# A decoder with a mixture of experts on one core: a second copy of late samples' rows for the scatter, joins of two samples at once, and the last products of the weights' quantization on GpSimd

## The chip, the core and the metric

The kernel runs on one core of a Trainium2 chip. Its engines are TensorE (PE, with PEld for its weight loads), VectorE (DVE), ScalarE (ACT), GpSimd (POOL) and SyncE (SP), which only issues DMAs. The metric is the device time of one execution in microseconds (us); the median of several runs counts.

## The reference, cut to what matters

Sixteen samples of 128 tokens x 256 features (f32) go through six sub-layers, with a layer norm after each. Only the last one is a mixture of experts; the change touches its routing, its output, and the preparation of the third one's weights.

```python
x = norm(x + L0_attn(x))         # a linear recurrence with decay per head
x = norm(x + L0_xattn(x, ctx))   # 16 heads, RoPE, softmax
x = norm(x + L0_ffn(x))          # weights and activations rounded to FP4 in blocks of 16
x = norm(x + L1_attn(x))         # linear attention, then a 1024-wide GELU network
x = norm(x + L1_xattn(x, ctx))   # 16 heads, softmax
x = norm(x + L1_ffn(x))          # 8 experts, the top 2 of each token:

probs = softmax(xf @ gate_w + gate_b)            # xf: 2048 x 256
gates, expert = top_k(probs, 2)
h = relu(xf @ w1[e] + b1[e])                     # 512 wide
expert_out = h @ w2[e] + b2[e]
out = sum over the two experts of gate * expert_out

def fp4_quant_dequant(x):                        # blocks of 16 values
    scale = max(|x|) / 6
    return nearest(x / scale in the grid 0, .5, 1, 1.5, 2, 3, 4, 6) * scale
```

## The kernel before

**Slots and the planner.** A sample lives in one of six slots (sample n in slot n % 6). The work of a sample is cut into pieces. Each piece names what it needs and gives its expected time on each engine (the functions `plan_*`; "D" is DVE, "A" and "a" are ACT, "P" and "p" are GpSimd, "S" is SP, "Q" and "L" are a DMA's time in the queue and its latency). When the program is built, a planner plays these pieces through greedily and writes down in which order each engine takes them. Each engine then runs its instructions strictly in that order, and waits on semaphores where an input isn't there. A changed cost or need in any `plan_*` can so move pieces of any sample on any engine.

**First stage.** The weights of the FP4 network are quantized in nine parts of 512 or 384 columns (`dve_weights`, `pool_weights`). For each, DVE finds the blocks' scales and rounds (L1062 is the small operation on the scales, 128x32); the last product with the scale goes to DVE for the five even parts (`dve_fp4_scale`, L1073) and to GpSimd for the four odd ones. Samples start while this goes on.

**Middle.** All engines work on several samples at a time. ACT's activations need function tables that are loaded on a change of function: L1447 is the exponential of attention, L1529 and L1534 belong to the GELU network, L1491 to the FP4 network's gate. An ACT_TABLE_LOAD in the trace or in the program order is such a change.

**Router.** For a sample n, PE transposes its finished rows X6, DVE and ACT make the softmax and the top 2, and PE counts ranks with two small matmuls (L988, L989); from these DVE makes two rows of destinations (`idx`, L1304), one for each expert. GpSimd then writes the 128 rows with an indirect DMA to `xs_d`, a buffer in HBM sorted by expert (`pool_router`, L1753). A row is 258 wide: 256 features, where its result has to go ("dest"), and its gate. For the second expert the same 128 rows are written again (`pool_second`, L1765), but dest and gate differ. Both copies would read the same tile X6, so GpSimd waits until the first scatter has landed, rewrites the two columns (L1762, L1763), and then issues the second.

**Expert tiles.** After samples 8, 12 and 16 a table says how many rows each expert has. The expert work is cut into tiles of 128 rows: 17 tiles are done between the samples' pieces and 22 behind the last table. A tile takes 1 MB of weights by two DMAs (L1899, L1903) and its rows by one (L1894), all issued by SP. On PE it is a transpose (`turn`, L710), an up product (8 x 128x128 matmuls in two chunks, L705 with EW as the second operand) and a down product (4 of 128x256). Eight weight loads of the last step are issued before its rows. They stand on SP behind the saving of sample 14 (`sp_bias`), which holds the gated b2 (L1359, a DVE add on X6, which has to wait until both scatters of the sample have read X6).

**Join.** When all tiles are stored, `join_turns` goes through the 16 samples: SP fetches 384 KB (two expert rows and x6 of each token, L1873), GpSimd adds the first (L1775), DVE adds the second (L1371) and computes mean and variance (L1373 to L1376), GpSimd takes the root (L1635), ACT centres and scales (L1598, L1602), SP writes the result (L1876).

## Time and profile before

| | us |
|---|---|
| three runs | 997.7, 997.95, 1003.37 |
| their median | 997.95 |
| the profiled execution | 995.66 |
| its span in the trace | 993.6 |
| busy in the span: PE, PEld | 869.8, 691.2 |
| busy: DVE, ACT, POOL | 619.7, 488.5, 289.8 |

The profiled execution took 2.1 us more than its span, and 2.3 us less than the median. The program has four stretches in the trace: the preparation to about 100 us, the samples with the first 17 tiles to about 840, the gap about the last sample's router to 872, and the last 22 tiles with the join behind them. PE is busy nine tenths and more of nearly every fortieth of the span but the first ones, the one at 845 to 870, and the last.

### The profile page before, as it was taken

How to read it: one execution, taken by the hardware profiler on the slowest of the kernel's cores; microseconds unless marked ns; L12 is line 12 of the kernel's file. 1: busy time of each engine (PE TensorE's matmuls, PEld its weight loads, DVE VectorE, ACT ScalarE, POOL GpSimd, SP SyncE). 2: the span in 40 equal slices, each digit the busy share in tenths (PEclk: the TensorE clock that was granted, in tenths of full speed). 3: DMA queues.
4: the chain of work that ended last, by engine and by line, in shares of the span. 5: the costliest groups of instructions: out<-in, count | busy, mean ns of one | idle time of the engine just before them, and what ended most of it. 6: DMA issues, size and time to landing. Idle time of an engine off the chain costs nothing.

```text
span 993.6 us, 19713 instructions
## 1 busy us (share of the span) xinstructions
PE 869.8 (88%) x7316; PEld 691.2 (70%) x7316; DVE 619.7 (62%) x1845; ACT 488.5 (49%) x1150; POOL 289.8 (29%) x473
## 2 busy tenths in 40 slices
PE   3569999989988989999999999999999999599950
PEld 2346777668766756767777887777677888489940
DVE  4999887674771798977755778767974444200016
ACT  1335545435446646455564555565444555145535
POOL 4313322111340143422121333322421123312236
PEclk9679999999998999999999999999999999889985
DMA  9996000000010000000000003321230036899836
GB/s 325 402 321 210 2 2 12 12 1 14 25 34 12 17 28 28 18 6 6 12 12 17 18 28 119 107 81 42 72 107 28 28 119 192 317 320 343 321 122 242
DMA packets 35950, 102.33 MB, mean 103 GB/s; under 512 B 4984, under 2 KB 20352, under 8 KB 35296
## 3 DMA queue, kind: packets, MB, share of 16 engines
q1 hardware_dynamic: 32448, 91.74, 27.1%
q0 software_dynamic: 3408, 9.34, 2.5%
q8 instruction: 58, 0.95, 0.4%
q14 instruction: 36, 0.29, 0.1%
HBM read 87.53 MB, written 33.35 MB: 122 GB/s over the span
## 4 chain that ended last, share of the span: by engine, by line
PE 70%; DVE 14%; ACT 6%; issue 4%; DMA 3%; POOL 2%; SPq 0%; ACTq 0%; DVEq 0%; POOLq 0%
PE ps L705 49%; PE ps L710 8%; PE ps L717 6%; PE ps L781 3%; DMA xs_d<-X,idx 2%; DVE PT L1109 2%; ACT PT L1447 2%; DVE stat L1045 1%; PE ps L848 1%; ACT slot_rows L1447 1%; PE ps L882 1%; DMA KB<-xs_d 1%; DVE sm L1061 1%; DVE PT L1096 1%; PE ps L891 1%
## 5 line engine op out<-in xcount | busy, mean ns | idle before, releaser
L1635 POOL TENSOR_TENSOR stat<-stat,mhalf 128x1 f32<-128x1 f32 x112 | 65.9, 589 | 322.3 <-DVE stat L1047 322.1
L705 PE MATMUL ps<-wall,slot_rows 128*128 128x256 f32 (+1 forms) x448 | 134.5, 425 | 10.1 <-ACT KB L1474 8.3
L705 PEld LDWEIGHTS ps<-wall,slot_rows 128*128 128x128 f32 x448 | 78.8, 194 | 32.7 <-issue 20.9
L1109 DVE TENSOR_REDUCE PT<-ps 128x8 f32<-128x1024 f32 x64 | 75.3, 1219 | 29.8 <-PE ps L717 29.8
L717 PE MATMUL ps<-KB 32*128 32x128 f32 (+1 forms) x2048 | 78.2, 290 | 10.4 <-ACT slot_rows L1447 3.5
L717 PEld LDWEIGHTS ps<-KB 32*128 32x128 f32 (+1 forms) x2048 | 66.0, 192 | 29.5 <-issue 25.7
L710 PE MATMUL ps<-cst,PT 128*128 128x128 f32 x512 | 75.5, 284 | 11.1 <-DVE PT L1109 4.1
L705 PE MATMUL ps<-wgu,slot_rows 128*128 128x352 f32 x256 | 81.0, 470 | 2.1 <-ACT PT L1452 0.8
L710 PEld LDWEIGHTS ps<-cst,PT 128*128 128x128 f32 x512 | 60.8, 146 | 27.3 <-issue 13.8
L705 PE MATMUL ps<-slot_rows,wall 128*128 128x128 f32 x640 | 78.4, 277 | 0.3 <-DVE slot_rows L1119 0.2
L705 PEld LDWEIGHTS ps<-slot_rows,wall 128*128 128x128 f32 x640 | 74.7, 192 | 4.0 <-issue 0.9
L705 PEld LDWEIGHTS ps<-wgu,slot_rows 128*128 128x128 f32 x256 | 48.4, 193 | 29.5 <-issue 3.3
L1409 ACT COPY slot_rows<-ps 128x256 f32<-128x256 f32 x96 | 35.7, 378 | 60.2 <-PE ps L710 59.8
L705 PE MATMUL ps<-wall,cT 128*128 128x512 f32 x128 | 64.3, 627 | 0.0
L705 PE MATMUL ps<-wall,PT 128*128 128x256 f32 x256 | 59.6, 386 | 1.7 <-ACT KB L1432 1.7
L705 PEld LDWEIGHTS ps<-wall,PT 128*128 128x128 f32 x256 | 48.3, 193 | 9.7 <-ACT KB L1432 2.0
L1701 POOL TENSOR_TENSOR KB<-PT,sm 128x352 f32<-128x352 f32 x32 | 26.1, 817 | 84.9 <-DVE PT L1069 84.7
L1045 DVE BATCH_NORM_STATS2 stat<-slot_rows 128x6 f32<-128x256 f32 x112 | 47.9, 428 | 3.8
L705 PE MATMUL ps<-wdn,PT 128*128 128x256 f32 x192 | 47.3, 388 | 0.0
L705 PE MATMUL ps<-EW,work 128*128 128x256 f32 x184 | 43.9, 381 | 2.4 <-DMA EW<-moe_w 1.4
L705 PE MATMUL ps<-work,EW 128*128 128x128 f32 x368 | 45.2, 276 | 0.9 <-DVE PT L1109 0.5
L705 PEld LDWEIGHTS ps<-work,EW 128*128 128x128 f32 x368 | 43.0, 192 | 1.6 <-DVE PT L1109 0.7
(237 smaller groups left out, 1803.8 us busy)
## 6 DMA issues: line engine op xcount, KB each, us to landing
EW<-moe_w SPq DMA_DIRECT2D x23, 514.0 KB, 4.2
EW<-moe_w SPq DMA_DIRECT2D x23, 512.0 KB, 5.1
PT<-moe_w SPq DMA_DIRECT2D x12, 514.0 KB, 5.5
PT<-moe_w SPq DMA_DIRECT2D x12, 512.0 KB, 6.5
wall<-wts SPq DMA_DIRECT2D x1, 4104.0 KB, 19.8
work<-xs_d SPq DMA_DIRECT2D x25, 129.0 KB, 2.7
KB<-ys_d SPq DMA_DIRECT2D x8, 384.0 KB, 6.2
slot_rows<-ys_d SPq DMA_DIRECT2D x8, 384.0 KB, 9.3
```

The source lines that it names most:

```text
L705: last = k.e.matmul(o, a, b, start=(i == 0), stop=(i == len(pairs) - 1))
L710: last = k.e.transpose(ps[:, u.at, c * P:(c + 1) * P], src[:, c * P:(c + 1) * P], ident)
L717: last = k.e.matmul(ps[:, at, c * P:(c + 1) * P], lhsT[lane, c * P:(c + 1) * P], rhs[lane, c * P:(c + 1) * P], start=True, stop=True)
L781: last = k.e.matmul(ps[lane:lane + HR, u.at, c:c + P], VS[:, s, h * (DH + 1):h * (DH + 1) + HR], exps(s, a, i // HC)[:, i % HC * P:(i % HC ...
L848: last = k.e.transpose(ps[0:kw[i], u.at + i // 4, (i % 4) * P:(i % 4 + 1) * P], KB[s][:, i * P:i * P + kw[i]], ident)
L882: last = k.e.matmul(o[:, c, :], AT[:, s, c * P:(c + 1) * P], V1(s)[:, c, :], start=True, stop=True)
L1045: k.after(k.step(e.bn_stats(v[:, 0:6], src)))
L1109: e.tensor_reduce(peak[:, 2 * p:2 * p + 2, :, DH], s4, AX.X, ALU.max).then_inc(emptied[u.at], 1)
L1409: k.e.copy(dst, v3(ps[:, u.at, 0:D], P)).then_inc(emptied[u.at], 1)
L1447: e.activation(v3(exps(s, a, p), 512), ps[:, u.at:u.at + 2, :], ACT.Exp, scale=DH ** -0.5).then_inc(emptied[u.at], 1)
L1635: return k.e.tensor_tensor(v[:, 7:8], v[:, 8:9], mhalf[:, :], ALU.pow)
L1701: e.tensor_tensor(h, y, bc(sm[:, s, j, 1, 0:m].unsqueeze(2), m, DH), ALU.mult).then_inc(gpsimd[s], 1)
```

## The change

It has three parts and a consequence.

1. **Weights.** GpSimd makes the last product of all nine parts; before it made four.

```diff
                 dve_fp4_head(k, part, width, tmp, small, wxn_ready)
                 yield
                 k.wait_ge(wabs_ready, i + 1)
-                if i % 2:
-                    dve_fp4_tail(k, tmp).then_inc(wy_ready, 1)
-                else:
-                    k.after(k.step(dve_fp4_tail(k, tmp)))
-                    dve_fp4_scale(k, part, width, tmp, small).then_inc(wq_even, 1)
+                dve_fp4_tail(k, tmp).then_inc(wy_ready, 1)
                 yield
...
         def pool_weights(k):
             for i, (f, lo, width) in enumerate(wq_parts):
                 yield
-                if i % 2:
-                    m = width // DH
-                    part, y = v3(raw[f][0][:, lo:lo + width], DH), v3(wq_part(i, width)[1], DH)
-                    k.wait_ge(wy_ready, i // 2 + 1)
-                    k.e.tensor_tensor(part, y, bc(ws[:, 1, 1, 0:m].unsqueeze(2), m, DH), ALU.mult).then_inc(wq_odd, 1)
+                m = width // DH
+                part, y = v3(raw[f][0][:, lo:lo + width], DH), v3(wq_part(i, width)[1], DH)
+                k.wait_ge(wy_ready, i + 1)
+                k.e.tensor_tensor(part, y, bc(ws[:, i % 2, 1, 0:m].unsqueeze(2), m, DH), ALU.mult).then_inc(
+                    wq_odd if i % 2 else wq_even, 1)
                 yield
```

2. **Router.** Samples 12 to 15 (TWIN) get a second copy of their row, in the space of slots 4 and 5 (`twin_rows`), which samples 10 and 11 (DONE) must have left. ACT copies the 256 features, GpSimd writes the two other columns, and both scatters are issued one behind the other. `pool_second` stays for samples 0 to 11. The copy of "dest" moves to the start of the router's work.

```diff
         def act_router(k):
             for n in range(B):
                 act_copy(k, U[n]["x6T"], x6T[:, :, :])
+                if n in TWIN:
+                    k.wait_ge(vector[slot(n)], count(VECTOR, n, "normed", 6))
+                    for m in DONE:
+                        k.wait_ge(vector[slot(m)], count(VECTOR, m, "normed", 6))
+                    k.e.copy(twin_rows(n)[:, 0:D], X6[:, slot(n), 0:D]).then_inc(twinned, 1)
                 yield
...
+        def pool_scatter(k, n, i, rows_):
+            k.e.indirect_dma_start(xs_d, bass.IndirectOffsetOnAxis(ap=idx[:, n, i:i + 1], axis=0), rows_,
+                                   None).then_inc(scattered[slot(n)], 16)
 
         def pool_router(k):
             for n in range(B):
-                yield
-                yield
-                yield
-                k.wait_ge(zeroed, 16 * len(zero_parts))
-                k.wait_ge(idx_ready, n + 1)
                 if n >= NS:
                     k.wait_ge(scattered[slot(n)], sent(n - NS))
                 k.e.tensor_copy(X6[:, slot(n), D:D + 1], k_("dest")[:, 2 * n:2 * n + 1]).then_inc(directed, 1)
+                if n in TWIN:
+                    for m in DONE:
+                        k.wait_ge(vector[slot(m)], count(VECTOR, m, "normed", 6))
+                    k.e.tensor_copy(twin_rows(n)[:, D:D + 1], k_("dest")[:, 2 * n + 1:2 * n + 2]).then_inc(twin_tail, 1)
+                yield
+                yield
+                if n in TWIN:
+                    k.wait_ge(picked, 2 * n + 1)
+                    k.e.tensor_copy(twin_rows(n)[:, D + 1:XW], mx8[:, n, 1:2]).then_inc(twin_tail, 1)
+                yield
+                k.wait_ge(zeroed, 16 * len(zero_parts))
                 k.wait_ge(directed, n + 1)
-                k.e.indirect_dma_start(xs_d, bass.IndirectOffsetOnAxis(ap=idx[:, n, 0:1], axis=0), X6[:, slot(n), :],
-                                       None).then_inc(scattered[slot(n)], 16)
+                k.wait_ge(idx_ready, n + 1)
+                pool_scatter(k, n, 0, X6[:, slot(n), :])
+                if n in TWIN:
+                    k.wait_ge(twinned, n - TWIN[0] + 1)
+                    k.wait_ge(twin_tail, 2 * (n - TWIN[0]) + 2)
+                    pool_scatter(k, n, 1, twin_rows(n))
                 yield
                 for t in step_at(n):
                     yield
```

3. **Join.** The 16 samples are joined in ten groups: six of two samples and four of one (samples 0, 7, 14, 15). GpSimd's add, DVE's add, the root and DVE's two small operations take a group at once; DVE's statistics and ACT's steps stay one for each sample. The buffer of statistics has a place for each sample.

```diff
+GROUPS = [range(0, 1), range(1, 3), range(3, 5), range(5, 7), range(7, 8), range(8, 10), range(10, 12), range(12, 14), range(14, 15),
+          range(15, 16)]
+
+TWIN = range(B - 4, B)
+DONE = range(B - 6, B - 4)
...
-            for what, n in join_turns():
+            for what, g in join_turns():
                 if what == "join":
-                    v, rows_ = mv2[:, n % 8, :], join_rows(n)
...
+                    n, (y1, y2, x6) = GROUPS[g], joined_rows(g)
+                    v = mv2[:, n[0]:n[-1] + 1, :]
+                    k.wait_ge(halved, g + 1)
+                    e.tensor_tensor(x6, x6, y2, ALU.add).then_inc(joined, 1)
+                    k.wait_ge(joined, g + 1)
+                    for i in range(len(n)):
+                        stats = k.step(e.bn_stats(v[:, i, 0:6], x6[:, i, :]))
+                    k.after(stats)
+                    for i in range(len(n)):
+                        aggr = k.step(e.bn_aggr(v[:, i, 6:8], v[:, i, 0:6]))
+                    k.after(aggr)
+                    e.tensor_scalar(v[:, :, 8:9], v[:, :, 7:8], 1e-5, None, ALU.add).then_inc(var6, 1)
+                    e.tensor_scalar(v[:, :, 6:7], v[:, :, 6:7], -1.0, None, ALU.mult).then_inc(var6, 1)
                 yield
...
                 if what == "add":
-                    rows_ = join_rows(n)
-                    x6 = rows_[:, 2 * D:3 * D]
-                    k.wait_ge(fetched[n], 16)
-                    k.e.tensor_tensor(x6, x6, rows_[:, 0:D], ALU.add).then_inc(halved, 1)
+                    y1, y2, x6 = joined_rows(g)
+                    for n in GROUPS[g]:
+                        k.wait_ge(fetched[n], 16)
+                    k.e.tensor_tensor(x6, x6, y1, ALU.add).then_inc(halved, 1)
                 elif what == "join":
-                    k.wait_ge(var6, 2 * n + 2)
-                    pool_root(k, mv2[:, n % 8, :]).then_inc(root6, 1)
+                    n = GROUPS[g]
+                    v = mv2[:, n[0]:n[-1] + 1, :]
+                    k.wait_ge(var6, 2 * g + 2)
+                    k.e.tensor_tensor(v[:, :, 7], v[:, :, 8], bc(mhalf[:, :], len(n)) if len(n) > 1 else mhalf[:, :],
+                                      ALU.pow).then_inc(root6, 1)
                 yield
```

4. **The planner's numbers** follow:

```diff
-        yield piece(work=[("D", 1.4, None), ("P", 1.2, ("wq", i)) if i % 2 else ("D", 0.7, ("wq", i))],
+        yield piece(work=[("D", 1.4, None), ("P", 1.2, ("wq", i))],
...
-        yield piece(0.25, [(n, "x6T")], [("A", 0.36, (n, "x6T"))], [(n, "done", 1)], True)
+        twin = n in TWIN
+        yield piece(0.25, [(n, "x6T")], [("A", 0.36, (n, "x6T")), ("p", 0.2 + 0.2 * twin, None), *[("a", 0.5, None)] * twin],
+                    [(n, "done", 1), *[(m, "done", 1) for m in DONE] * twin], True)
...
-        yield piece(work=[("D", 2.05, (n, "routed"))], needs=[("f", n - 2, "gT")] * (n > 1))
-        yield piece(0.4, [(n, "rank")], [("D", 0.78, (n, "rank")), ("P", 1.16, None), ("Q", 0.5, None),
-                                         ("L", 2.4, (n, "half sent"))])
+        yield piece(work=[("D", 2.05, (n, "routed")), *[("p", 0.2, None)] * twin], needs=[("f", n - 2, "gT")] * (n > 1))
+        yield piece(0.4, [(n, "rank")], [("D", 0.78, (n, "rank")), ("P", 1.0, None), ("Q", 0.5, None),
+                                         ("L", 2.4, (n, "half sent"))] if n not in TWIN else
+                    [("D", 0.78, (n, "rank")), ("P", 1.9, None), ("Q", 0.5, None), ("L", 2.6, (n, "sent"))])
         for t in step_at(n):
...
 def plan_second():
-    for n in range(B):
+    for n in range(TWIN[0]):
         yield piece(work=[("P", 1.4, None), ("Q", 0.5, None), ("L", 2.4, (n, "sent"))], needs=[(n, "half sent")], alone=True)
```

Since these feed the planner, the order of the instructions changes on all engines. On ACT the program had 49 ACT_TABLE_LOADs and has 61. One place of it, before (L1529 and L1534: GELU network; L1447: attention's exponential; L1464, L1441, L1409, L1421: copies that need no table of their own):

```order
L1529 ACT_TABLE_LOAD
L1529 ACTIVATE PT<-ps,col 128x128 x8
L1464 ACTIVATE slot_rows<-ps,col 128x128 x2
L1534 ACTIVATE slot_rows<-slot_rows 128x256
L1529 ACTIVATE PT<-ps,col 128x128 x8
L1441 COPY KB<-ps 128x512
L1409 COPY slot_rows<-ps 128x256 x2
L1421 COPY VS<-ps 128x16x16
L1534 ACTIVATE slot_rows<-slot_rows 128x256
L1447 ACT_TABLE_LOAD
```

After (the lines have moved: L1543 and L1548 are the GELU network, L1461 the exponential):

```order
L1548 ACTIVATE slot_rows<-slot_rows 128x256
L1461 ACT_TABLE_LOAD
L1461 ACTIVATE PT<-ps 128x1024
L1461 ACTIVATE slot_rows<-ps 128x1024
L1543 ACT_TABLE_LOAD
L1543 ACTIVATE PT<-ps,col 128x128 x8
L1461 ACT_TABLE_LOAD
L1461 ACTIVATE PT<-ps 128x1024
L1461 ACTIVATE slot_rows<-ps 128x1024
L1466 COPY PT<-ps 128x512
L1423 COPY slot_rows<-ps 128x256
L1435 COPY VS<-ps 128x16x16
```

Four changes of table stand where one stood: GELU pieces and exponentials alternate.

PE about the last sample's router, before. The transpose of X6 is that of sample 15, "x6T 128x8" its logits, L988 and L989 its ranks; "work,EW" is an up product and "EW,work" a down product of an expert tile:

```order
L710 MATMUL ps<-cst,X6 128x128 x2
L1000 MATMUL ps<-cst,gates 8x128
L705 MATMUL ps<-work,EW0 128x128 x8
L705 MATMUL ps<-wall,x6T 128x8 x2
L705 MATMUL ps<-EW1,work 128x256 x4
L710 MATMUL ps<-cst,work 128x128 x2
L988 MATMUL ps<-mask,cst 128x8
L989 MATMUL ps<-mask,ones 128x8
L705 MATMUL ps<-work,EW1 128x128 x8
L705 MATMUL ps<-EW0,work 128x256 x4
L705 MATMUL ps<-work,EW0 128x128 x8
L1006 MATMUL ps<-b2m,gT 128x256
```

After (L726 is L705, L731 is L710, L1009 and L1010 are the ranks); the first pair of ranks is sample 14's, the second sample 15's:

```order
L1009 MATMUL ps<-mask,cst 128x8
L1010 MATMUL ps<-mask,ones 128x8
L731 MATMUL ps<-cst,X6 128x128 x2
L1021 MATMUL ps<-cst,gates 8x128
L726 MATMUL ps<-EW1,work 128x256 x4
L726 MATMUL ps<-wall,x6T 128x8 x2
L731 MATMUL ps<-cst,work 128x128 x2
L726 MATMUL ps<-work,EW1 128x128 x8
L726 MATMUL ps<-EW0,work 128x256 x4
L1009 MATMUL ps<-mask,cst 128x8
L1010 MATMUL ps<-mask,ones 128x8
L726 MATMUL ps<-work,EW0 128x128 x8
```

One more up product and one more down product of expert tiles stand ahead of the last ranks (the 8 x 128x128 and the 4 x 128x256 ones that were behind them).

GpSimd for samples 14 and 15, before ("X6<-cst" writes dest, "X6<-mx8" the gate):

```order
L1751 COPY X6<-cst 128x1
L1753 DMA xs_d<-X6,idx 19200x258
L1787 DMA ys_d<-work,place 7168x256
L1762 COPY X6<-cst 128x1
L1763 COPY X6<-mx8 128x1
L1765 DMA xs_d<-X6,idx 19200x258
L1751 COPY X6<-cst 128x1
L1753 DMA xs_d<-X6,idx 19200x258
L1787 DMA ys_d<-work,place 7168x256
L1762 COPY X6<-cst 128x1
L1763 COPY X6<-mx8 128x1
L1765 DMA xs_d<-X6,idx 19200x258
```

After (L1765 is now every scatter; L1772, L1776 and L1781 write the columns):

```order
L1765 DMA xs_d<-X6,idx 19200x258
L1765 DMA xs_d<-slot_rows,idx 19200x258
L1772 COPY X6<-cst 128x1
L1776 COPY slot_rows<-cst 128x1
L1825 DMA ys_d<-work,place 7168x256
L1781 COPY slot_rows<-mx8 128x1
L1825 DMA ys_d<-work,place 7168x256
L1765 DMA xs_d<-X6,idx 19200x258
L1765 DMA xs_d<-slot_rows,idx 19200x258
```

Between a sample's two scatters there is nothing now, and the copies that write the columns stand ahead of them.

## Rows read from the trace of the kernel before

**Rows 1.** Windows (busy us of PE, PEld, DVE, ACT, POOL; PEclk, DMA share, GB/s).
```profile
14.00:100.00 86.00, 58.48 (x424) 40.29 (x428) 75.09 (x162) 32.64 (x70) 24.63 (x37) 0.84 0.90 323
100.00:840.00 740.00, 705.50 (x6209) 554.76 (x6210) 507.99 (x1525) 387.45 (x862) 205.38 (x352) 0.99 0.13 40
840.00:872.00 32.00, 17.69 (x110) 14.84 (x109) 8.64 (x51) 7.41 (x26) 9.97 (x15) 0.87 0.81 285
```

**Rows 2.** Timeline of DVE, first stage: start us, length us, engine, line.
```profile
26.80 0.69 DVE L1073 TENSOR_TENSOR EW<-work,X 128x512 f32<-128x512 f32 x1
...
28.12 0.18 DVE L1062 TENSOR_SCALAR X<-X 128x32 f32<-128x32 f32 x1
...
32.44 0.84 DVE L1062 TENSOR_SCALAR X<-X 128x32 f32<-128x32 f32 x1
```

**Rows 3.** Lines of ACT: the largest of six groups of table loads.
```profile
L1447 ACT ACT_TABLE_LOAD x17 | 21.8, 1283 | 11.8 <-PE ps L717 11.6
```

**Rows 4.** Waits of PE from 100 to 840, on ACT: us, times, longest us.
```profile
PE ps L710 <- ACT PT L1447: 5.6, 4, 1.9
...
PE ps L891 <- ACT PT L1529: 0.2, 1, 0.2
```

**Rows 5.** Timeline of ACT around one table load.
```profile
305.81 1.02 ACT L1447 ACTIVATE slot_rows<-ps 128x1024 f32<-128x1024 f32 x1
306.85 1.28 ACT L1529 ACT_TABLE_LOAD   x1
```

**Rows 6.** Timeline of PE at the last router, and where it restarts.
```profile
846.55 0.36 PE L988 MATMUL ps<-mask,cst 128*128 128x8 f32 x2 [0.77 <-DVE mask L1288]
...
847.29 2.02 PE L705 MATMUL ps<-work,EW 128*128 128x128 f32 x16 [0.16 <-DMA EW<-moe_w]
849.15 1.89 PE L705 MATMUL ps<-EW,work 128*128 128x256 f32 x8
...
871.35 1.09 PE L710 MATMUL ps<-cst,KB 128*128 128x128 f32 x4 [11.98 <-DMA KB<-xs_d]
```

**Rows 7.** Timeline of DVE: the add before sample 14 is saved.
```profile
854.11 0.42 DVE L1359 TENSOR_TENSOR X<-X,ps 128x256 f32<-128x256 f32 x1 [2.16 <-DMA xs_d<-X,idx]
```

**Rows 8.** Timeline of GpSimd: sample 15's two scatters.
```profile
851.34 0.98 POOL L1753 DMA_INDIRECT xs_d<-X,idx  x1 [0.28 <-POOL X L1751]
...
856.96 0.98 POOL L1765 DMA_INDIRECT xs_d<-X,idx  x1 [0.28 <-POOL X L1763]
```

**Rows 9.** Timeline of SP's issues: first early weight load; first rows of a tile.
```profile
855.64 0.34 SPq L1899 DMA_DIRECT2D PT<-moe_w  x1
...
864.60 2.53 SPq L1894 DMA_DIRECT2D KB<-xs_d  x3
```

**Rows 10.** DMA issues from 864.5 to 864.8: KB each, median us to landing.
```profile
KB<-xs_d SPq DMA_DIRECT2D x1, 129.0 KB, 6.6
```

**Rows 11.** Lines of the stretch 960 to 994, shapes apart.
```profile
L1635 POOL TENSOR_TENSOR mv<-mv,mhalf 128x1 f32<-128x1 f32 x16 | 9.8, 609 | 2.7 <-DVE mv L1376 2.6
...
L1775 POOL TENSOR_TENSOR slot_rows<-slot_rows 128x256 f32<-128x256 f32 x8 | 5.7, 719 | 0.0
...
L1373 DVE BATCH_NORM_STATS2 mv<-slot_rows 128x6 f32<-128x256 f32 x8 | 3.4, 428 | 0.3
...
L1371 DVE TENSOR_TENSOR KB<-KB 128x256 f32<-128x256 f32 x8 | 3.4, 421 | 28.0 <-POOL KB L1775 28.0
...
L1374 DVE BATCH_NORM_AGGREGATE mv<-mv 128x2 f32<-128x6 f32 x16 | 2.9, 182 | 0.6
```

**Rows 12.** Timeline of DVE: its last instruction.
```profile
986.71 0.14 DVE L1376 TENSOR_SCALAR mv<-mv 128x1 f32<-128x1 f32 x1
```

**Rows 13.** Tile ys_d from 950 to 994: the fetches' issues, and landings.
```profile
L1873 SPq DMA_DIRECT2D KB<-ys_d x8: 332/430/759, 960.5 to 963.7; - x8
L1873 SPq DMA_DIRECT2D slot_rows<-ys_d x8: 430/478/706, 964.5 to 968.5; - x8
...
DMA to landing us min/median/max: 2.4/7.5/11.0
```

95 lines of the change are left out of this document (46 added, 49 removed).

## The prediction

> **What bounds the kernel now.** I read the windows first, cut where the work changes its kind. From 14 to 100 us DVE is busy for 75.09 of 86 us and PE for 58.48 only: the preparation hangs on DVE. From 100 to 840 PE is busy for 705.50 of 740 us, at a granted clock of 0.99 (the 2.4 GHz level nearly throughout), with ACT at 387.45: PE bounds this stretch, and all that others can cost or give there is what they make PE wait. From 840 to 872 PE has 17.69 of 32 us [rows 1], and one wait of 11.98 us for the rows of an expert tile stands at its end [rows 6]. So the change touches four places with four different limits: DVE at the start, PE's small idle time in the middle, a chain of router, scatter and loads in the gap, and the join, where PE has nothing left and DVE and GpSimd alternate.
>
> **Weights: DVE's products go to GpSimd.** One product on DVE takes 0.69 us for 512 columns [rows 2]. Five go, the last of 384 columns, so 4 x 0.69 + 0.52 = 3.3 us of DVE work, and DVE is the engine that counts. But the traces show a price: the small operation on the scales, L1062, takes 0.18 us behind a DVE product and 0.84 us when it runs beside GpSimd's product of the part before [rows 2]. After the change it runs beside one four times more: 4 x (0.84 - 0.18) = 2.6 us back. Net **-0.7 us**. The ends are -3.3 (no such stall) and +1.0 (stalls also on the next operation, and GpSimd's product being slower than DVE's for the matmuls that wait for the weights); I take the middle one, since it is the same operation in the same loop.
> The Trainium skill has a rule against this part: "GPSIMD Engine Reference", Key points, says that GpSimd and VectorE share their interfaces to SBUF, so that work given from one to the other isn't free. The 0.84 us agree with it; by it alone the gain would be about nil, as in the upper half of my range.
>
> **The middle: order and table loads.** Of the three parts only the twins' copies can run there (four of 128x256 on ACT, which has half of its time free, and small ones on GpSimd); I cost them at nothing. But the planner orders everything anew, and the program's order on ACT has 61 table loads in place of 49, 12 more. One costs 1.283 us of ACT [rows 3], so 12 x 1.283 = 15.4 us of ACT's time, which has 740 - 387 = 353 us free. What counts is what PE waits. PE's waits for ACT in this stretch are 15 rows, the first with 5.6 us and the last with 0.2, and add up to 22.1 us [rows 4]. Not each is due to a load, but if I put all on the 49 loads, one costs PE 22.1 / 49 = 0.45 us, and 12 cost **+5.4 us**. The ends are 0 (all hidden, PE has other samples' work) and +15.4 (each in front of a piece that PE waits for; what speaks for it is that the new loads stand in front of exponentials, and the exponentials' line leads PE's waits [rows 4]). I take 5.4, nearer to the low end, because PE idles for only 34.5 us in this stretch with 49 loads that last 63 us: on average most are covered. A reorder can also gain: PE's other 12 us of idle time are its waits for DVE and DMA, and I see no reason for them to move either way.
> For the price of one load, the row shows 1.28 us, and the activation before it ends at 306.83 and the load starts at 306.85 [rows 5]: the engine doesn't empty first. The Trainium skill says otherwise. "ScalarE: Activation LUTs", What ACT_TABLE_LOAD costs, gives 1283 ns for the load and about as much again for the drain before it, some 2.66 us, and its next section tells one to batch work by table set, which this order goes against. By the page the 12 would be an estimated 31.9 us of ACT.
>
> **The last router.** Before, the chain is: sample 15's ranks at 846.55 [rows 6]; idx, and GpSimd's first scatter at 851.34; GpSimd waits for its landing, copies the two columns and issues the second at 856.96 [rows 8]. DVE meanwhile waits 2.16 us for sample 14's second scatter before the add at 854.11 [rows 7], SP saves the result and can issue the eight early weight loads, from 855.64 on; the first rows of a tile are asked for at 864.60 [rows 9] and land 6.6 us later [rows 10], at 871.2, and PE starts at 871.35 [rows 6]. The rows can't be asked for before the scatters have landed (856.96 + some 6 = 863 to 864), and they land behind the weights that were asked for first.
> What the change takes off: sample 14's two scatters go together, so DVE's wait of 2.16 us before the add goes [rows 7], and SP's queue starts that much earlier; for sample 15 the second scatter can be issued when the first has been, after 0.98 us: 856.96 - (851.34 + 0.98) = 4.6 us earlier [rows 8]. What it adds: PE's order now has one more up product (2.02 us) and one more down product (1.89 us) ahead of the last ranks, 3.91 us [rows 6]. All that hangs on the ranks moves by that.
> Which of the two savings counts? The weights of four tiles, 4 MB, were asked for between 855.64 and 864, and the DMA engines are busy for 0.81 of this stretch [rows 1]. I take it that the landing hangs on when this traffic starts, so 2.16 is saved and not 4.6: 3.91 - 2.16 = **+1.8 us**. The ends are -4.6 (the scatter was what counted, and the ranks aren't later, since PE now fills its wait of 0.77 us and DVE's top 2 is what decides) and +3.9 (nothing of the scatters counts). Then what is late is the same DMA, later.
>
> **The join.** Before, each sample takes DVE an add of 0.42, statistics of 0.43, their sum of 0.18 [rows 11] and two small operations of 0.14 [rows 12], 1.31 us, and GpSimd a root of 0.61 and an add of 0.72, 1.33 us [rows 11]. They alternate with small gaps between them. The fetches were issued until 968.5 and the last landed up to 11.0 us later, at 979.5 [rows 13]; DVE ended at 986.85 [rows 12], so the join is behind the fetches by the end, and its pace counts. After: a pair takes DVE one add of 512 columns (0.69, as the product of this size [rows 2]), 2 x 0.43, 2 x 0.18 and 2 x 0.15, 2.2 us in place of 2.6, and GpSimd 0.61 + 1.1 = 1.7 in place of 2.7. DVE then has some 1.1 us a sample, about what a fetch takes to land (the first by about 962.9, 960.5 plus the shortest 2.4, so (979.5 - 962.9) / 15 = 1.1 us apart [rows 13]). Samples 12 and 13 have landed at 979.5 - 2.2 = 977.3; the pair's add ends by 978.6, DVE's part at 980.8; the single 14 ends 1.33 later, at 982.1, and 15 at 983.45. 986.85 - 983.45 = **-3.4 us**. The ends are -5.3 (only the last fetch counts: 979.5 + 0.72 + 1.33 = 981.55) and -1.0 (the pairs gain only the gaps, 0.16 us for each of six, and wait for their second fetch).
>
> **The sum.** -0.7 + 5.4 + 1.8 - 3.4 = +3.1 us. The profiled execution took 995.66 us, 2.1 over its span; that stays. 998.8 by it; the median of the three runs is 2.3 above the profiled one, so **1001 us**. With the middle's nearer ends the own range of this case is 995 to 1008.
>
> **Rivals.**
> *Hidden loads.* All 12 lie beside PE's work. For it: ACT is free for half of the stretch, and the planner knows no idle PE here. Against it: PE waits for ACT 25 times already [rows 4]. -0.7 + 1.8 - 3.4 = -2.3: 995.7.
> *It does what it says.* The loads are hidden and the second scatter was what held the rows: -0.7 - 4.6 - 3.4 = -8.7, so 989.3. For it: the rows are asked for within a microsecond of the second scatter's landing [rows 8, 9]. Against it: the two products ahead of the ranks, and 6.6 us for 129 KB that can't be all its own time [rows 10].
> *Slower: the exponentials wait.* The place is ACT between GELU pieces and exponentials in the middle. Each extra load delays an exponential that PE's next transpose waits for. It decides from the point where PE has no other sample's matmuls ready, since PE takes its pieces in a fixed order. Then -0.7 + 15.4 + 1.8 - 3.4 = +13.1: 1011.
> *The page's price.* If a switch costs ACT twice what the load shows and PE pays it all, by mechanism the engine's pipeline has to empty at each of the 12 places: 2 x 15.4 = 30.8 us, +28.5, 1026. The trace has no such gap [rows 5]. The Trainium skill's page above is the one that says so.
>
> **Chances.** The forecast 0.42, hidden loads 0.24, it does what it says 0.14, exponentials wait 0.14, the page's price 0.03, something else 0.03. The range from 989 to 1011 reaches to the two outer cases and leaves out about half of each and the last two, some 2 in 10. A measurement of this kernel can tell about 1%, 10 us, from no change. Below 988 lies nearly half of the third case and a bit of the second: 0.12. Above 1008 the exponentials' case, the page's and a tail of the first: 0.17. Within: 0.71.
>
> **What the profile after would show.** The weights: nine products of GpSimd, none of DVE, and L1062's successor at 0.8 us nine times rather than four; DVE's busy time before 100 us down by a microsecond at most. The loads: 61 of them, and PE's idle time between 100 and 840 at 40 us in place of 34.5; at 34 or less the loads were hidden, at 50 the third rival is right. The router: from the last ranks to the first early weight load 7 us in place of 9.1, the ranks 4 us later against PE's tiles, and PE's wait at the restart at 10 to 14 us; at 8 or less the scatters were what counted. The join: DVE's last instruction 3.4 us nearer to PE's end, and pairs about 2.1 us apart.
> **What would make it wrong.** The order is new in every stretch; a wait that neither trace nor order shows me in the middle, of ten samples' pieces meeting otherwise, can be larger than all four terms. It would show as PE idle time on DVE or on DMAs there.

## The result, and the profile after

The changed kernel takes 1005.62 us (median of 17 runs, 1002.72 to 1011.09), the kernel before 997.26 us on the same chips (17 runs). The ratio is **1.0081**, with a 95% interval from 1.0066 to 1.0095: 8 us slower, less than 1%, more than the interval. The profiled execution took 1006.35 us, 10.7 more than that of before; its span is 1004.5.

The windows of the changed kernel, the same stretches as [rows 1] and the next one:

```profile
14.00:100.00 86.00, 60.94 (x421) 41.96 (x422) 72.70 (x157) 32.56 (x69) 27.59 (x38) 0.82 0.90 323
100.00:840.00 740.00, 695.47 (x6103) 543.93 (x6103) 498.67 (x1495) 398.64 (x859) 205.00 (x352) 0.99 0.11 36
840.00:872.00 32.00, 29.25 (x213) 25.04 (x211) 14.98 (x76) 13.35 (x46) 14.30 (x21) 1.00 0.69 226
```

Between 100 and 840 us PE is busy for 10 us less than before (695.47 for 705.50, idle for 44.5 in place of 34.5), and the gap for the last router comes later. The clock in this stretch is as before (0.99). So the time is lost in the middle. PE and SP at the last router and the restart (timelines; start us, length us):

```profile
861.81 0.28 PE L1009 MATMUL ps<-mask,cst 128*128 128x8 f32 x2
...
862.62 2.02 PE L726 MATMUL ps<-work,EW 128*128 128x128 f32 x16 [0.30 <-DMA EW<-moe_w]
...
883.32 1.08 PE L731 MATMUL ps<-cst,KB 128*128 128x128 f32 x4 [13.77 <-DMA KB<-xs_d]
```
```profile
868.65 0.34 SPq L1938 DMA_DIRECT2D PT<-moe_w  x1
...
875.49 2.54 SPq L1933 DMA_DIRECT2D KB<-xs_d  x3
```

The last ranks come at 861.81, 15.3 us later than in [rows 6]; the first early weight load stands 6.84 us behind them, before 9.09 [rows 6, 9]; PE restarts 21.5 us behind them, before 24.8. From the restart to the first fetch of the join it is 88.5 us in place of 89.1 (971.85 - 883.32; 960.5 - 871.35), from there to the end of the span 32.65 in place of 33.1. That adds up: 15.3 - 3.3 - 0.6 - 0.5 = 10.9, the difference of the spans.

What is in the 15.3? The windows from 100 us to the last ranks, of before and then of the changed kernel:

```profile
100.00:846.50 746.50, 711.27 (x6249) 559.83 (x6249) 510.95 (x1544) 390.86 (x875) 207.59 (x355) 0.99 0.13 41
```
```profile
100.00:861.80 761.80, 717.27 (x6273) 563.15 (x6274) 508.63 (x1546) 409.32 (x896) 214.47 (x367) 0.99 0.13 41
```

PE is idle for 761.8 - 717.3 = 44.5 us, before for 35.2: 9.3 more. It is busy for 6.0 more, of which 3.9 are the up and the down product that now stand ahead of the ranks; no further matmuls stand behind the other 2.1 (the 24 more records, 16 and 8, are those two products). The waits of PE on ACT are 32.7 us in 37 instances (before 22.1 in 25); these are the largest of them (us, times, longest us), and they answer to [rows 4]:

```profile
PE ps L726 <- ACT PT L1461: 9.3, 7, 2.9
PE ps L802 <- ACT PT L1461: 5.3, 2, 2.8
PE ps L731 <- ACT PT L1461: 5.1, 5, 2.1
```

L1461 is the exponential.

The join on GpSimd, from 970 us on (groups by line, shapes apart; count, busy us, mean ns; idle before):

```profile
L1815 POOL TENSOR_TENSOR mv<-mv,mhalf 128x2 f32<-128x2 f32 x6 | 6.1, 1013 | 1.2 <-DVE mv L1390 1.2
L1810 POOL TENSOR_TENSOR slot_rows<-slot_rows 128x512 f32<-128x512 f32 x3 | 3.9, 1291 | 0.0
L1810 POOL TENSOR_TENSOR KB<-KB 128x512 f32<-128x512 f32 x3 | 3.8, 1259 | 2.7 <-DMA KB<-ys_d 2.7
L1815 POOL TENSOR_TENSOR mv<-mv,mhalf 128x1 f32<-128x1 f32 x4 | 2.2, 557 | 0.9 <-DVE mv L1390 0.9
```

A root of two columns takes 1.01 us where one takes 0.56, and an add of 512 columns 1.29: 2.3 us of GpSimd for a pair, 1.15 for a sample, before 1.33 [rows 11]. The first pairs wait 2.7 us for their fetches. From the add of sample 3 to that of sample 14 it is then 13.7 us (980.27 to 993.98), before 15.6 (967.86 to 983.49). Here is how DVE and GpSimd meet in one pair (two timelines):

```profile
983.37 0.71 DVE L1389 TENSOR_SCALAR mv<-mv 128x2 f32<-128x2 f32 x1
```
```profile
982.80 1.25 POOL L1810 TENSOR_TENSOR KB<-KB 128x512 f32<-128x512 f32 x1
984.23 1.11 POOL L1815 TENSOR_TENSOR mv<-mv,mhalf 128x2 f32<-128x2 f32 x1 [0.18 <-DVE mv L1390]
```

DVE's small operation takes 0.71 us here and 0.18 in the next pair; it ends at 984.08, just behind the end of GpSimd's add at 984.05, and the root waits for it.

The preparation (timeline of DVE, one line of GpSimd; L1083 is what L1062 was):

```profile
27.64 0.54 DVE L1083 TENSOR_SCALAR X<-X 128x32 f32<-128x32 f32 x1
...
32.31 0.84 DVE L1083 TENSOR_SCALAR X<-X 128x32 f32<-128x32 f32 x1
...
49.50 0.69 DVE L1089 SCALAR_TENSOR_TENSOR work<-work 128x512 f32<-128x512 f32 x1 [1.04 <-ACT work L1427]
```
```profile
27.09 1.06 POOL L1758 TENSOR_TENSOR EW<-work,X 128x512 f32<-128x512 f32 x1 [3.45 <-DVE work L1090]
```

The same place on DVE in the kernel before:

```profile
49.51 0.73 DVE L1068 SCALAR_TENSOR_TENSOR work<-work 128x512 f32<-128x512 f32 x1 [0.55 <-ACT work L1413]
```

Each of the four products of 512 columns that left DVE frees 0.73 us (26.07 to 26.80 in the trace of before, start to start), and L1083 takes 0.36 of it back: 0.54 in place of 0.18. It ends at 28.18, again just behind the end of GpSimd's product at 28.15. What is left of the gain goes at 49.5: DVE comes there earlier, but waits for ACT 1.04 us in place of 0.55, and starts at the same time. Between 14 and 100 us DVE's busy time falls by 2.4 us (72.70 for 75.09), where the prediction had a microsecond at most.

### The profile page after: what moved, and what is told of

Its sections match the earlier page's. It is cut to its first block, busy times and chain, and to the rows that moved or that the text cites. A ratio compares the mean times of both kernels' runs of the same rounds, so it can differ in the third digit from the quotient of the medians.

```text
span 1004.5 us, 19682 instructions
## 1 busy us (share of the span) xinstructions
PE 873.9 (87%) x7316; PEld 692.2 (69%) x7316; DVE 613.0 (61%) x1822; ACT 505.0 (50%) x1166; POOL 294.6 (29%) x466
## 4 chain that ended last, share of the span: by engine, by line
PE 65%; DVE 18%; ACT 8%; issue 5%; DMA 2%; POOL 1%; SPq 1%; ACTq 0%; DVEq 0%; POOLq 0%
PE ps L726 46%; PE ps L731 8%; PE ps L738 6%; PE ps L802 3%; ACT PT L1461 2%; DVE PT L1125 1%; DVE stat L1066 1%; ACT slot_rows L1461 1%; PE ps L869 1%; DVE PT L1090 1%; ACT L1461 1%; DVE sm L1082 1%; DMA KB<-xs_d 1%; PE ps L912 1%; DVE KB L1186 1%
## 5 line engine op out<-in xcount | busy, mean ns | idle before, releaser
L1657 POOL TENSOR_TENSOR stat<-stat,mhalf 128x1 f32<-128x1 f32 x112 | 68.0, 608 | 316.8 <-DVE stat L1068 316.6
L726 PE MATMUL ps<-wall,slot_rows 128*128 128x256 f32 (+1 forms) x448 | 134.8, 428 | 18.0 <-ACT KB L1488 9.2
L726 PEld LDWEIGHTS ps<-wall,slot_rows 128*128 128x128 f32 x448 | 79.7, 195 | 42.0 <-issue 21.1
L731 PE MATMUL ps<-cst,PT 128*128 128x128 f32 x512 | 76.1, 286 | 11.2 <-DVE PT L1125 4.5
L726 PE MATMUL ps<-slot_rows,wall 128*128 128x128 f32 x640 | 79.5, 278 | 3.8 <-ACT slot_rows L1478 1.9
L726 PE MATMUL ps<-wgu,slot_rows 128*128 128x352 f32 x256 | 80.0, 462 | 1.8 <-DVE PT L1125 1.3
L726 PEld LDWEIGHTS ps<-slot_rows,wall 128*128 128x128 f32 x640 | 75.2, 192 | 9.1 <-ACT slot_rows L1478 2.9
L731 PEld LDWEIGHTS ps<-cst,PT 128*128 128x128 f32 x512 | 61.3, 147 | 25.5 <-issue 15.8
L726 PE MATMUL ps<-wall,cT 128*128 128x512 f32 x128 | 66.4, 645 | 1.6 <-ACT PT L1461 1.6
L726 PEld LDWEIGHTS ps<-wgu,slot_rows 128*128 128x128 f32 x256 | 47.4, 190 | 27.3 <-issue 2.1
L726 PE MATMUL ps<-wall,PT 128*128 128x256 f32 x256 | 58.3, 381 | 3.8 <-ACT PT L1461 2.2
L1423 ACT COPY slot_rows<-ps 128x256 f32<-128x256 f32 x96 | 36.0, 380 | 46.5 <-PE ps L731 46.4
L726 PEld LDWEIGHTS ps<-wall,PT 128*128 128x128 f32 x256 | 47.4, 190 | 11.0 <-ACT PT L1466 2.6
L726 PE MATMUL ps<-wdn,PT 128*128 128x256 f32 x192 | 48.3, 394 | 0.0
L726 PE MATMUL ps<-work,EW 128*128 128x128 f32 x368 | 45.5, 277 | 1.7 <-ACT PT L1461 1.4
L726 PEld LDWEIGHTS ps<-work,EW 128*128 128x128 f32 x368 | 42.9, 192 | 2.8 <-ACT PT L1461 1.7
L1543 ACT ACTIVATE PT<-ps,col 128x128 f32<-128x128 f32 x128 | 36.2, 372 | 16.6 <-PE ps L726 16.2
```

Source lines behind the costliest of these rows:

```text
L726: last = k.e.matmul(o, a, b, start=(i == 0), stop=(i == len(pairs) - 1))
L731: last = k.e.transpose(ps[:, u.at, c * P:(c + 1) * P], src[:, c * P:(c + 1) * P], ident)
L1423: k.e.copy(dst, v3(ps[:, u.at, 0:D], P)).then_inc(emptied[u.at], 1)
L1543: ins = e.activation(hT[:, i, :], ps[:, u.at, j * P:(j + 1) * P], ACT.Gelu, bias=c_("b1")[:, i:i + 1])
L1657: return k.e.tensor_tensor(v[:, 7:8], v[:, 8:9], mhalf[:, :], ALU.pow)
```

## The experiments

The twelve kernels ran in three sets of four, each kernel 5 to 12 times, and each ratio is to the 23 to 29 runs of before on the same chip in the same set. The traces are of one execution each. Two questions: which part costs or gains, and what it is about the new order.

### The parts in the order of before

The planner decides the order from its costs, so a part can be built in with the old costs, where a new piece of work costs the planner nothing. For the weights:

```diff
-        yield piece(work=[("D", 1.4, None), ("P", 1.2, ("wq", i))],
+        yield piece(work=[("D", 1.4, None), *([("P", 1.2, ("wq", i))] if i % 2 else [("D", 0.7, ("wq", i)), ("p", 0.0, None)])],
```

and likewise for the router's columns and copies ("p", 0.0 and "a", 0.0, for the twins only; the copy of "dest" moves only for them).

**All three parts.** 

> All three parts of the change, with the order of the kernel before: the planner keeps the old costs (new pieces cost it nothing), so PE, ACT and SP keep their order but for a few pieces at the last two routers, and ACT has 49 table loads. Theory A, the order costs: the slowdown is gone, and what the parts gain is left: 0.65 us by the weights, 3.3 between the last ranks and PE's restart, 0.4 in the join, 4.4 us in all, a ratio to the kernel before of 0.9956, and about 0.988 to the changed one. Theory B, the new instructions cost (GpSimd's products beside DVE, twins' copies on ACT, roots of two columns): the slowdown stays, ratio 1.004 to 1.008. In between, with the last ranks' place on PE as the cause: 1.000.

Measured 0.9999 (0.9988 to 1.0010), 995.55 us. So the 8 us are the order's: with the same instructions in nearly the old order they are gone (the two products stand ahead of the last ranks here too). The trace shows where. The window from 100 us to its last ranks:

```profile
100.00:848.60 748.60, 716.67 (x6273) 564.16 (x6274) 512.54 (x1546) 393.52 (x884) 210.62 (x363) 0.98 0.13 42
```

These are the same 6273 matmuls as in the changed kernel, and PE is busy as long (716.7 for 717.3), but it is idle for 31.9 us in place of 44.5. Of these 12.6 us, 11.3 are waits for ACT (21.4 in place of 32.7). The gain of 4.4 us that I expected beside it did not come.

**The weights' part.** 

> Only the weights' part: all nine last products on GpSimd, everything in the order of before. Theory A: DVE gains 4 x 0.61 us of products and pays 4 x 0.36 for L1062's successor beside GpSimd's product, about 0.6 to 1.0 us less, ratio 0.999 to 1.000. Theory B: contention with GpSimd takes it all back and more, 1.001 to 1.003.

Measured 1.0005 (0.9996 to 1.0014). Nothing is gained that can be measured. Of 0.73 us for each product, 0.36 go in the stall of L1083. Of the other 1.5 us in all, 0.7 go in two longer waits for ACT, as in the rows above (in this run's trace 0.92 us at 49.1, before 0.55, and 1.06 at 67.9, before 0.72). At the last part DVE is 0.8 us earlier (69.78 for 70.59), and the time of the run doesn't show it.

**The join's part.** Its diff is GROUPS and what hangs on it; with GROUPS of one sample each the code is that of before. 

> Only the join's part: groups of two; all else, the order too, is that of before. Theory A (GpSimd paces the pairs: an add of 1.26 and a root of 1.1 us each): 0.4 us less, as in the changed kernel, ratio 0.9996, inside the noise. The prediction's term would be 3.4 us less, 0.9966. Rival: it is slower, since a pair waits for its second fetch before GpSimd starts: 1.001.

Measured 0.9996 (0.9988 to 1.0005). The prediction's 3.4 us (0.9966) are outside of the interval.

**The router's part.** 

> Only the router's part (twins of samples 12 to 15), the planner with the old costs: 49 table loads, the order of before but for some 20 rows of PE at the last routers (an up and a down product stand ahead of sample 15's ranks, as in the changed kernel). Theory: 3 us less between the last ranks and PE's restart, and 2 to 3 us more ahead of the ranks, so nothing: ratio 0.999 to 1.000. Rival, the twins' copies on ACT cost PE something in the middle: 1.002. By the prediction's term, +1.8 us: 1.0018.

Measured 1.0038 (1.0016 to 1.0060), 3.8 us slower, more than the 0.999 to 1.000 that I expected, though each scatter goes at once; the 1.0018 by the prediction's term is inside of the interval. The interval from the last ranks to PE's restart is 21.7 us, before 24.8, but the ranks come at 853.1 in place of 846.55. Of these 6.5 us, 3.9 are the two products. Another 2 come 20 us earlier, at a place that has no wait in the kernel before (ACT and PE):

```profile
832.51 0.58 ACT L1470 COPY PT<-ps 128x512 f32<-128x512 f32 x1 [3.12 <-remote]
```
```profile
833.15 0.66 PE L730 MATMUL ps<-cst,PT 128*128 128x128 f32 x4 [1.98 <-ACT PT L1470]
```

"remote" stands in the view where no instruction of the core is found as the releaser. DVE too sits idle until 832.57. The trace of all three parts in the old order has no such pause. Whether every execution has it isn't known, so some of the 3.8 us may not be the twins' at all. The next run takes the rest apart.

**Only the last ranks moved.** In the kernel before the planner is told that sample 15's top 2 takes 2 us more, which moves the two rows of the ranks on PE and puts a store of GpSimd ahead of the last scatters:

```diff
-        yield piece(work=[("D", 2.05, (n, "routed"))], needs=[("f", n - 2, "gT")] * (n > 1))
+        yield piece(work=[("D", 2.05 + 2.0 * (n == B - 1), (n, "routed"))], needs=[("f", n - 2, "gT")] * (n > 1))
```

> The kernel before with one thing moved: on PE the ranks of sample 15 stand behind one more up and one more down product of expert tiles, as in the changed kernel; nothing else changes on PE, ACT, DVE and SP (GpSimd has one store ahead of the last scatters). By the prediction's term it costs 3.9 us, ratio 1.0039. If the weights' traffic and not the ranks set the restart: 1.000.

Measured 1.0023 (1.0007 to 1.0039): 2.3 us slower, and there is no twin in it; the 3.9 us of the prediction's term are at the end of the interval. PE from the two products to the restart, SP's first early weight load, DVE's add, and the second scatter of sample 15 (four timelines):

```profile
847.70 2.53 PE L705 MATMUL ps<-work,EW 128*128 128x128 f32 x16 [1.85 <-DMA EW<-moe_w]
850.02 3.10 PE L705 MATMUL ps<-EW,work 128*128 128x256 f32 x8
852.96 0.28 PE L988 MATMUL ps<-mask,cst 128*128 128x8 f32 x2
...
875.01 1.09 PE L710 MATMUL ps<-cst,KB 128*128 128x128 f32 x4 [13.10 <-DMA KB<-xs_d]
```
```profile
859.72 0.34 SPq L1899 DMA_DIRECT2D PT<-moe_w  x1
```
```profile
858.20 0.41 DVE L1359 TENSOR_TENSOR X<-X,ps 128x256 f32<-128x256 f32 x1
```
```profile
860.72 0.98 POOL L1765 DMA_INDIRECT xs_d<-X,idx  x1 [0.28 <-POOL X L1763]
```

And the second scatter in the changed kernel, with its twin:

```profile
865.81 0.96 POOL L1765 DMA_INDIRECT xs_d<-slot_rows,idx  x1 [0.30 <-issue]
```

The ranks come 6.4 us later than before and not 3.9: PE waits for the first product's weights, and the products take longer (2.53 and 3.10 us for 2.02 and 1.89). The load stands 6.76 us behind the ranks and the restart 22.05, close to the kernels with twins (6.84 and 21.5 in the changed one). DVE's add no longer waits for sample 14's second scatter, where it waited 2.16 us before [rows 7], simply because the ranks of sample 15, from which the table is made, come later and the scatter has landed by then. So the 2 to 3 us between ranks and restart that the changed kernel is better by come with the delay of the ranks itself. The twins add little: they bring the second scatter from 7.76 us behind the ranks (860.72 - 852.96) to 4.00 (865.81 - 861.81), 3.8 us earlier, and the restart comes half a microsecond earlier. The run with the weights' own costs, below, has no twins either and restarts 20.7 us behind its ranks (874.94 - 854.21). For scale: the runs of the weights and of the join in the old order, where nothing was changed here, have 23.7 and 23.9 in place of 24.8.

### What it is about the order

**Twelve more table loads in the old order.** One exponential is put into the middle of the GELU work of six samples:

```diff
                 for j in range(4):
                     i = 4 * m + j
+                    if n in (3, 5, 7, 9, 11, 13) and m == 0 and j == 2:
+                        e.activation(idle1[:, :], c_("b1")[:, 0:1], ACT.Exp)
                     ins = e.activation(hT[:, i, :], ...
```

> The kernel before with one exponential of 128x1 put between the second and the third GELU activation of samples 3, 5, 7, 9, 11 and 13, whose result nobody uses. This makes 12 more table loads (61, as in the changed kernel) with the order of everything else unchanged. By the sum's term they cost 5.4 us, ratio 1.0054. If each costs PE what it costs ACT: 15.4 us and 6 x 0.2 for the exponentials, 1.016. If PE hides them: 1.000. If the changed kernel's slowdown is the loads and not the rest of the order, it should be about the 10.6 us by which PE's waits on ACT grew: 1.0106.

Measured 1.0205 (1.0192 to 1.0219), above all that I expected: 20.4 us for 12 loads, 1.7 us each, more than a load lasts and far more than my 0.45. One of the places, on ACT and then on PE:

```profile
240.87 1.28 ACT L1531 ACT_TABLE_LOAD   x1
242.16 0.20 ACT L1531 ACTIVATE idle<-col 128x1 f32<-128x1 f32 x1
242.37 1.28 ACT L1532 ACT_TABLE_LOAD   x1
243.67 1.66 ACT L1532 ACTIVATE PT<-ps,col 128x128 f32<-128x128 f32 x6
```
```profile
238.25 3.73 PE L706 MATMUL ps<-slot_rows,wall 128*128 128x128 f32 x32
244.35 0.44 PE L711 MATMUL ps<-cst,slot_rows 128*128 128x128 f32 x2 [2.36 <-ACT PT L1532]
244.62 4.64 PE L706 MATMUL ps<-wdn,PT 128*128 128x256 f32 x12
```

The same 12 matmuls in the kernel before, and the window of this run behind the wait:

```profile
242.56 2.95 PE L705 MATMUL ps<-wdn,PT 128*128 128x256 f32 x12
```
```profile
244.90:248.30 3.40, 3.40 (x10) 2.54 (x8) 0.00 (x0) 0.69 (x3) 0.00 (x0) 0.50 0.00 0
```

No gap stands ahead of the second load (242.16 + 0.20 = 242.36). PE waits 2.36 us, and then the 12 matmuls behind it take 4.64 us in place of 2.95: the clock has fallen to 1.2 GHz (0.50). The DMA engines move nothing at that time (share 0.00), so they have no part in this fall. Over the stretch from 100 us to the last ranks:

```profile
100.00:866.70 766.70, 720.19 (x6237) 566.14 (x6231) 510.52 (x1542) 408.15 (x893) 207.63 (x355) 0.97 0.13 39
```

PE is idle for 46.5 us (before 35.2) and busy for 720.2 (before 711.3). The lost time is half waiting, 11.3 us (0.9 for each load), and half slower matmuls, 8.9.

**Fewer loads, and another order.** Two runs with a part's own costs in the planner.


> Only the router's part, with its own costs in the planner: the order moves on all engines and ACT has 45 table loads, 4 fewer than before. Theory A, table loads decide what an order costs: 4 x 0.9 = 3.5 us less than the router's part in the old order, ratio 0.996. Theory B, any new order loses what a tuned one had, by waits of many kinds: 1.003 to 1.010, like the changed kernel.

Measured 1.0131 (1.0107 to 1.0156), with 45 loads, above both theories: 0.996 by the count of loads (A), 1.003 to 1.010 by any new order (B).

> Only the weights' part, with its own costs in the planner: the order moves on all engines and ACT has 58 table loads, 9 more than before. Theory A: 9 x 0.9 = 8 us more, ratio 1.008. Theory B, the new order as such: 1.003 to 1.010 too, so this run tells the theories apart only together with the one of 45 loads.

Measured 0.9997 (0.9981 to 1.0013), with 58 loads, where both theories had it slower, 1.003 to 1.010. The number of table loads does not decide: the order with the fewest is the slowest, the one with 9 more than before costs nothing. The windows from 100 us to the last ranks, of the router's run and of the weights':

```profile
100.00:868.00 768.00, 733.04 (x6307) 577.81 (x6307) 509.03 (x1544) 391.30 (x887) 213.30 (x365) 0.97 0.13 43
```
```profile
100.00:854.20 754.20, 719.65 (x6307) 565.39 (x6305) 510.51 (x1547) 402.89 (x895) 214.84 (x366) 0.99 0.14 44
```

Both have three down and two up products more ahead of the last ranks than the kernel before, both are idle for 35 us, like before. But the first is busy for 13.4 us more than the second with the same 6307 matmuls: the granted clock is 0.97 for 0.99. So PE's idle time in sum doesn't tell what an order costs either; it counts where the waits lie. One of the falls (windows), and PE's waits around it (timeline):

```profile
590.00:596.00 6.00, 4.45 (x36) 2.76 (x37) 5.14 (x15) 2.18 (x4) 2.06 (x5) 1.00 0.13 45
596.00:600.00 4.00, 2.27 (x34) 1.58 (x26) 0.42 (x1) 3.40 (x5) 0.00 (x0) 1.00 0.37 78
600.00:605.00 5.00, 4.90 (x96) 4.19 (x96) 2.36 (x2) 1.69 (x3) 0.00 (x0) 0.61 0.80 283
605.00:610.00 5.00, 4.30 (x46) 3.79 (x42) 3.01 (x5) 0.95 (x3) 0.00 (x0) 0.50 0.40 158
610.00:615.00 5.00, 5.00 (x31) 4.55 (x27) 2.42 (x3) 1.23 (x4) 0.00 (x0) 0.52 0.16 41
```
```profile
592.59 0.66 PE L730 MATMUL ps<-cst,PT 128*128 128x128 f32 x4 [1.07 <-DVE PT L1115]
593.73 1.13 PE L725 MATMUL ps<-wall,slot_rows 128*128 128x256 f32 x4 [0.48 <-DVE PT L1124]
600.10 1.22 PE L737 MATMUL ps<-KB 16*128 16x128 f32 x32 [1.83 <-ACT slot_rows L1465]
```

Three waits close together, 3.4 us, and then the clock is at 1.2 GHz (0.50) nearly until 615, though PE is busy. That these waits bring the fall is read from their order in time, here and in the run with added loads; no run took them away alone.

**All parts with 45 loads.** 

> All three parts, with the planner told nothing of the weights' and the router's new costs but the twins' needs: the order of the router's part by itself, 45 table loads. Theory A: 0.996 as that run, less 0.4 us in the join: 0.995 to 0.996, which would beat both kernels. Theory B: 1.003 to 1.010.

Measured 1.0137 (1.0105 to 1.0168): the router's order again, with the same clock of 0.97 in the middle (34.3 us idle, 731.3 busy). Theory A, that the number of table loads is what an order costs, has fallen. The same three parts have now run in three orders, at 0.9999, 1.0081 and 1.0137.

**The loads ahead of the waits.** A load stands behind the semaphore wait of the activation that needs it, so it starts when the operand is there: ACT is idle for 11.8 us before the 17 loads of [rows 3], 11.6 of it ended by PE. Here a small activation of the new function goes ahead of the wait:

```diff
+        table = ["Exp", 0]
+
+        def warm(k, n, func):
+            if table[0] != func and n > 1:
+                k.e.activation(idle1[:, table[1] % 16:table[1] % 16 + 1], c_("b1")[:, 0:1], getattr(ACT, func))
+                table[1] += 1
+            table[0] = func
...
                 u = u_["prob", a, p]
+                warm(k, n, "Exp")
                 k.wait_ge(filled[u.at], u.full)
```

(the same ahead of the Silu, the GELUs and the router's exponential; nobody uses its result).

> The kernel before, with its table loads moved ahead of the waits: wherever ACT's function changes, an activation of 128x1 with the new function (its result unused) stands ahead of the wait for the operand, so that the load runs while ACT waits. 49 loads as before, order unchanged, 0.2 us more of ACT for each. If loads inside PE's waits are what an order costs: PE's waits on ACT with a load inside them were 13.6 us of 22.1, with 6.0 us at most of load time in them, so 3 to 6 us less, ratio 0.995. If the loads' place behind the wait doesn't matter: 1.000, or 1.002 by the small activations.

Measured 0.9979 (0.9968 to 0.9990), 2 us less, below the 3 to 6 that I expected. PE's waits on ACT in the trace are 19.8 us, before 22.1.

> The changed kernel with its 61 loads moved ahead of the waits in the same way. In it PE's waits on ACT with a load inside were 20.6 us of 32.8, 7.0 more than before. If these carry the slowdown, 7 to 10 us go and the ratio to the kernel before is 0.998 to 1.002. If the loads were only near by and the order costs otherwise, it stays at 1.006 to 1.009.

Measured 1.0061 (1.0047 to 1.0074), against 1.0081 without it. In both kernels the medians fall by 2 us; in the changed one that isn't clear of noise, as the two intervals overlap (1.0047 to 1.0074, 1.0066 to 1.0095). So the load's place behind its wait explains at most a small part of the difference between the two. PE's waits on ACT are still 31.7 us in the trace of the changed kernel with it, and its idle time up to the last ranks is 44.3 us, without it 44.5; what is shorter in its trace is PE's busy time (712.1 for 717.3). ACT is then late with its queue, with or without a load in the wait; what makes it late at each place was not tried.

**The fastest.** Weights (own costs in the planner), join in groups, loads ahead of the waits, no twins.


> The parts without the router's: weights with their own costs in the planner (58 loads, which measured 0.9997 by itself), the join in groups (0.9996), and the loads ahead of the waits. If the three add up: 0.9997 - 0.0004 - 0.005 = 0.994, the fastest version so far.

Measured 0.9960 (0.9948 to 0.9972), 993.0 us against 996.47 of before on the same chip. It beats both kernels, by 0.4% and 1.2%. It is short of the 0.994 that I expected, but that sum held 0.005 for the loads ahead of their waits. With the measured 0.9979 the parts add up to 0.9972, and the run is at or below that. Its window up to the last ranks shows where part of that lies:

```profile
100.00:847.80 747.80, 715.06 (x6307) 562.62 (x6305) 511.18 (x1547) 410.12 (x949) 215.53 (x366) 1.00 0.14 44
```

These are the 6307 matmuls of the weights' order, at a clock of 1.00 for 0.99: PE is busy for 4.6 us less (715.1 for 719.7), and idle for 32.7.

## Why the forecast came out, and where its steps did not

The forecast was 1001 us from 997.95, 0.3% slower, with a range from 989 to 1011; the kernel became 0.8% slower. The side and the range hold. Of the four terms, the largest was right in its place (PE waiting for ACT in the new order) and wrong in its price, one was right in parts that can't be added as I did, and two were gains that are not there. So the side is in part luck: I came to it by counting table loads, and the count isn't what an order costs. The router's order, with 4 loads fewer than before, would by the same working have been forecast no slower than before, and is 1.3% slower. (The range is given as 989 to 1011, the chances beside it are worked out for 988 to 1008; 1005.6 lies in both.)

- **Middle, +5.4 us.** "PE's waits for ACT" is the right place and the largest term, as put: they grew by 10.6 us, and PE's idle time between 100 and 840 us is 44.5, where I had 40. That the order costs, and not the instructions, is shown: 0.9999 with the old order, and 31.9 us idle for 44.5 with the same matmuls up to the last ranks. What failed is the working, 12 more loads at an average of 0.45 us. An average over 49 loads says nothing of 12 others: 12 loads cost 20.4 us where PE waits behind them, and 9 more in another order cost nothing. Of the changed kernel's 37 waits on ACT, 12 have a table load inside them or one that ended less than 0.2 us ahead, 20.6 us together, before 9 with 13.6. So 7 of the 10.6 us are in waits with a load; that the loads cause them is not shown, since moving the loads ahead of the waits gave back only 2.
- **Last router, +1.8 us.** The 3.91 us of the two products are there, and so are the 2.16 us, in the interval to the first weight load (9.09 to 6.84). But I gave the 2.16 to the twins, and the run with only the ranks moved has them too: a later table finds the scatter landed. So the term's sum is a cost of the delay and a gain of the same delay, and the twins stand in neither. The router's part in the old order, twins and delayed ranks together, costs 3.8 us, the delay without twins 2.3, with intervals that overlap. The rival "it does what it says", with 4.6 us by the second scatter, is wrong: with that scatter 3.8 us nearer to the ranks, the restart comes 0.5 us nearer. Twins without the products ahead of the ranks weren't tried, as the planner moved the ranks whenever the twins were there.
- **Join, -3.4 us.** It measured -0.4 (0.9996). I took DVE as the pace and GpSimd's pair at 1.7 us, with a root of 0.61 for two columns as for one. The root of two takes 1.01 to 1.11 and the add 1.26: 2.3 us, and with the 0.2 us for which the root waits for DVE, whose small operation ends only with GpSimd's add, two of the pairs take 2.5 where two samples took 2.8 (adds at 980.27, 982.80 and 985.31; before at 973.42 and 976.24). From sample 3 to 14 this gains 1.9 us in all; 0.9 go at the start, where the first pair waits for two fetches, and 0.5 at the end, behind the last pair's root. The smallest gain in my range was 1.0, which was still too much.
- **Weights, -0.7 us.** I took the stall as 0.66 us, from the first of the places in the trace of before; at the next two, and at the four new ones, it is 0.36. By the same sum this makes 3.3 - 1.4 = 1.9 us of gain, but in the changed kernel's trace DVE is only 0.4 us earlier at the seventh part than before (56.51 for 56.92): it started 0.25 later and waits longer for ACT. As a run it is 1.0005: no gain that can be measured. What the term left out is DVE's wait for ACT.
- **"The page's price".** No drain stands ahead of a load (305.81 + 1.02 to 306.85 before, 242.16 + 0.20 to 242.37 in the run with added loads), and none behind it (242.37 + 1.28 to 243.67). The 2.66 us that the Trainium skill gives ("ScalarE: Activation LUTs", What ACT_TABLE_LOAD costs) are not what ACT pays; each load here lasts the page's 1283 ns, and nothing more. What PE pays for a load in its way, 1.7 us, is 0.9 of waiting and 0.7 of slower matmuls.

What stays open: the three parts in the old order measured 1.0005, 0.9996 and 1.0038 one by one and 0.9999 together, 4 us less than they add up to. In the traces PE's idle time up to the last ranks is 31.9 us against 36.4 in the router's run, at the same busy time (716.7). Nearly all waits are the same ones, one for one. The router's run has 1.98 us more at 833, by the pause of ACT and DVE whose cause the profile doesn't show, and 0.76 ahead of the last ranks. At 295 it waits 2.40 us for 0.76, but there the matmuls ahead of the wait took 1.88 for 3.32, so nothing is lost by it. And which waits make the changed order worse than the weights' order, with almost as many table loads, is seen (ACT's exponentials) but not tried piece by piece.

## What to carry to other kernels

Where a planner orders all engines from a table of costs, every edit of a cost is two changes: build each part once with the old order (new work at cost nothing), and the part's own worth is seen apart from the luck of the new order. Here the same three parts cost 0, 8 and 14 us in three orders. Count what stands ahead of the one instruction on which a gap hangs, and ask what else its delay brings with it, before a saving is put down to the edit that was meant for it. And a cost of an operation taken as an average over all its places is no price for a new place.

## What the runs showed of the hardware

Waits of PE can cost more than themselves. In the run with 12 added loads, 11.3 us of waiting came with 8.9 us of slower matmuls; one wait of 2.36 us had the clock at 1.2 GHz behind it. In the router's own order the idle time was that of the weights' order, and the granted clock's fall from 0.99 to 0.97 alone made 13.4 us.

On GpSimd a power of 128x2 takes 1.01 us against 0.56 for 128x1: a second column costs nearly as much as the first.

A small operation of DVE beside a GpSimd operation on 512 columns ended only with it, at most 0.05 us behind its end: L1083 at 28.18 (GpSimd's product at 28.15) and L1389 at 984.08 (GpSimd's add at 984.05). So its length is set by when it meets the other, 0.54 or 0.84 us in place of 0.18 for the one, and 0.71 for the other.
